# Graph attention and expert layer on one core: tile numbers turned on TensorE, x loaded first, tiles ranked, expert results scattered plainly into two halves and joined at the end

## The chip, the cores and the metric

The kernel runs on one core of one Trainium2 chip. The metric is the device time of one execution in microseconds (us); lower is better. The engines of the core are PE (TensorE, with its weight loads shown as PEld), DVE (VectorE), ACT (ScalarE), POOL (GpSimd) and SP (SyncE, which here only starts DMAs). Each engine works through its own instructions in order, and they wait for each other with semaphores.

## The reference, cut to what matters

6250 nodes with 256 features, 200000 edges sorted by destination. Two graph attention layers (4 heads, then 1), added to x, then a mixture of 8 experts of which each node takes its best two.

```python
def _gat_layer(x, src, dst, W, a_src, a_dst, b, heads, concat):
    h = (x @ W).reshape(n, heads, -1)
    e = jax.nn.leaky_relu(al_s[src] + al_d[dst], NEG_SLOPE)
    ex = jnp.exp(e - m[dst])                      # m: maximum per destination
    alpha = ex / (denom[dst] + 1e-16)             # denom: sum of ex per destination
    out = jax.ops.segment_sum(h[src] * alpha[:, :, None], dst, num_segments=n)
...
x = x + gnn(_layernorm(x), ...)                   # two such layers, elu between them
# ffn of _layernorm(x): probs = softmax(xf @ gate_w + gate_b); top 2 of 8 experts
cw = zeros((N, 8)).at[arange(N)[:, None], top2_idx].add(top2_vals)
for each expert:  h = gelu(xf @ w1 + bb1); y = h @ w2 + bb2; acc = acc + we[:, None] * y
return x + acc
```

## The kernel before

The 6250 nodes are 49 tiles of 128 rows (NT = 49), the last of which has 106 (LAST). The 200000 edges are cut into windows of 128. An item is one window for one node tile; ITEMS = 1616 items are worked off in STEPS = 202 steps of 8. The phases follow one another, each in a block of its own that all engines leave together.

**start_phase.** For each node tile SP loads a tile of x into one of SETS = 4 places of `xt`, DVE norms it (`begin_norm`, `end_norm`), PE turns it (`turn_tile`) and multiplies it by the weights (`multiply`), ACT copies the product into `acc` and POOL stores it into a table in DRAM. Between the tiles stands the edge plan. SP first copies `dst` and `src` into DRAM tables of windows, and reads the first node number of each window into `first`. At t = PLAN_AT = 2 DVE folds the second layer's weights and runs `make_plan` in one piece: how many windows begin below each tile (`below`, `count`, summed on PE), where each tile's windows begin and end, and from a comparison over 13 x 49 numbers (`cmp`) each item's tile (`tile_i`) and window (`win_i`), with items in the order of the tile numbers. SP stores `tile_i` to DRAM in 13 transfers of one column each, 128 numbers of 4 bytes, after the load for tile 6. POOL gathers the windows of 128 items at a time (`raw`), and at every third tile from t = 6 (BLOCK_AT) DVE, PE and ACT turn such a block.

**edge_phase** (twice). In a step POOL gathers 8 times 128 table rows by source node, DVE, ACT and PE weigh them and sum them by destination, and DVE adds each item's sum to its tile of `acc`. Steps run over the items in the order of the plan.

**route_norm_phase, route_phase.** The node values after the graph layers (`mid_tile`) are stored to DRAM into the later part of the tensor `back`, normed values stay in `acc`. The best two experts of each node give it two slots. POOL sends each node's row of `acc` twice to the slots' rows of the DRAM tensor `sent`: 256 values, the row number of its home in `back`, and its share (the gate's weight).

**expert_phase.** 106 slot tiles (SLOT_TILES) of 128 rows, each of one expert. SP loads a tile (`xe`); PE turns it (`turn_x`), multiplies it with the expert's first weights (`up`), turns the result (`turn_h`) and multiplies again (`down`). In PE's order tile k's `turn_h` is followed by `down` of tile k - 1. `up` and `down` begin with reading the number of the tile's expert from SBUF into a register (`value_load`, line 1595), from which the weights' address is worked out. DVE adds the biases (`bias_h`, `bias_y`), copies (`copy_h`), and finds the homes and shares (`find_home`, in rings of 8 columns). ACT does gelu (`gelu`, line 1720), copies the turned x (`copy_x`, 1716) and multiplies the result by the share (`weigh_y`, 1726). In ACT's order `weigh_y` of tile k - 1 stands between `copy_x` of tile k + 2 and `gelu` of tile k + 1. POOL scatters each result tile to its homes in `back` with a DMA that adds to what is there; each such store waits for the one before it to have landed, as a node has two.

**combine_phase.** One DMA copies 6250 rows of `back` to the output.

## Time and profile before

| | |
|---|---|
| runs of the kernel before | 5241.19, 5238.65, 5240.36 us; median 5240.36 |
| the profiled execution | 5236.12 us, with a span of 5234.5 us in the trace |
| start phase | 0 to about 125 us |
| first edge phase | about 160 to 2290 us |
| second edge phase | about 2420 to 4355 us |
| routing | about 4355 to 4680 us |
| expert phase | about 4687 to 5206 us |
| the copy to the output | 5212.4 to 5234.5 us |
| busy, of the span | PE 69%, POOL 65%, DVE 65%, ACT 28% |

A busy share over the whole span says little here, since the phases have different limits: within a phase one asks which engine never waits for long, and what ends the waits of the others. DMA work is not an engine's busy time. The chain of work that ended last is given at the end of the page; here it names PE's matmuls of the expert phase.

### The profile page before, as it was taken

The numbers are of one execution on the slowest core, as the hardware profiler recorded it, in microseconds if no ns is written. First come the engines' busy times: TensorE is split into PE (matmuls) and PEld (weight loads), VectorE is DVE, ScalarE is ACT, GpSimd is POOL, SyncE is SP. The second block draws the span as 40 slices with busy tenths as digits, with TensorE's granted clock in tenths as the row PEclk, the third lists the DMA queues.
The fourth block names the chain that finished last, engine by engine and source line by source line (L and its number), as shares of the span: only waits on it lengthen the run. The fifth ranks groups of instructions, "written<-read, shape, count | busy, mean of one in ns | idle before, by whom it ended". The sixth has DMA issues, their size and how long they took to land. (4 is left out here: it accounts for less than half of the span.)

```text
span 5234.5 us, 76220 instructions
## 1 busy us (share of the span) xinstructions
PE 3631.5 (69%) x12542; PEld 2230.4 (43%) x12543; DVE 3422.5 (65%) x8917; ACT 1488.3 (28%) x3315; POOL 3424.8 (65%) x3626
## 2 busy tenths in 40 slices
PE   5477777777777777757777777777777774219996
PEld 4244444444444444434444444444444443206664
DVE  5677777777777777776777777777766776504442
ACT  3222222222222222342222222222222222103232
POOL 4577777777777777537777777777777772353332
PEclk8677777777777878777777777777777776559998
DMA  5344444444444444325555555555555555123334
GB/s 138 108 132 132 133 133 132 133 133 134 133 133 132 133 133 133 94 90 139 138 138 139 138 138 139 139 139 139 139 138 138 139 136 162 69 79 56 55 56 87
DMA packets 298785, 644.90 MB, mean 123 GB/s; under 512 B 74539, under 2 KB 132779, under 8 KB 298322
## 3 DMA queue, kind: packets, MB, share of 16 engines
q0 software_dynamic: 183376, 475.89, 34.8%
q1 hardware_dynamic: 106882, 156.45, 10.8%
q10 hardware_dynamic: 8480, 12.06, 0.7%
q14 instruction: 34, 0.28, 0.0%
q8 instruction: 13, 0.21, 0.0%
HBM read 583.32 MB, written 68.80 MB: 125 GB/s over the span
## 5 line engine op out<-in xcount | busy, mean ns | idle before, releaser
L999 POOL DMA_INDIRECT rows<-table,idx x3232 | 3055.9, 946 | 1025.7 <-issue 919.8
L1072 PE MATMUL bank<-rows,hit 128*128 128x260 f32 (+1 forms) x6464 | 2620.7, 549 | 1080.7 <-DVE acc L1134 1065.3
L1072 PEld LDWEIGHTS bank<-rows,hit 128*128 128x128 f32 x6464 | 1467.1, 256 | 2031.7 <-DVE acc L1134 1778.2
L1134 DVE TENSOR_TENSOR acc<-acc,bank 128x260 f32 (+1 forms) x3232 | 1356.0, 420 | 180.4 <-issue 34.9
L1125 DVE TENSOR_TENSOR rows<-rows,bank 128x1024 f32<-128x1024 f32 x808 | 946.3, 1212 | 1.3 <-ACT rows L1032 1.3
L1029 ACT ACTIVATE arg<-arg 128x32 f32<-128x32 f32 (+1 forms) x404 | 88.4, 219 | 2833.7 <-DVE arg L1118 2833.7
L1111 DVE TENSOR_TENSOR arg<-rows,bank 128x32 f32<-128x32 f32 (+1 forms) x404 | 71.6, 177 | 999.9 <-DMA rows<-table,idx 999.9
L1092 DVE TENSOR_TENSOR hit<-bank,dst_loc 128x256 f32<-128x256 f32 x1616 | 672.9, 417 | 0.1
L1023 ACT ACTIVATE hit_t<-gap,ones 128x1024 bf16<-128x1024 bf16 x404 | 464.0, 1148 | 20.7
L1018 ACT ACTIVATE gap<-loc,minus_node 128x1024 bf16<-128x1024 bf16 x404 | 462.6, 1145 | 10.2 <-DMA loc<-loc_row 6.3
L1061 PE MATMUL bank<-du,hit_t 128*128 x3232 | 375.1, 184 | 119.6 <-ACT hit_t L1023 80.0
L1061 PEld LDWEIGHTS bank<-du,hit_t 128*128 128x128 bf16 x3232 | 297.6, 103 | 344.0 <-issue 253.0
L1585 POOL DMA_INDIRECT back<-ye,xe_home x106 | 163.9, 1546 | 352.6 <-ACT ye L1726 240.0
L1631 PE MATMUL bank<-fw,hidt 128*128 x848 | 212.2, 394 | 30.7 <-issue 30.6
L1612 PE MATMUL bank<-fw,xet 128*128 x424 | 206.1, 609 | 1.6 <-ACT xet L1716 1.6
L1631 PEld LDWEIGHTS bank<-fw,hidt 128*128 128x128 f32 x848 | 153.6, 191 | 71.9 <-issue 54.9
L1677 DVE TENSOR_TENSOR ye<-bank,fb 128x256 f32<-128x256 f32 x106 | 45.0, 425 | 179.5 <-PE bank L1631 179.5
L1663 DVE TENSOR_TENSOR hid<-bank,fb 128x512 f32<-128x512 f32 x106 | 73.3, 692 | 125.9 <-PE bank L1612 125.9
L1602 PE MATMUL bank<-ident,xe 128*128 128x128 f32 x212 | 40.8, 275 | 155.2 <-DMA xe<-sent 155.2
L1726 ACT ACTIVATE ye<-ye,xe_share 128x256 f32<-128x256 f32 x106 | 53.8, 508 | 315.1 <-DVE ye L1677 315.1
L1439 POOL DMA_INDIRECT sent<-acc,slot x98 | 95.6, 976 | 59.1 <-issue 29.2
L1246 POOL DMA_DIRECT2D back<-mid_tile x49 | 26.5, 541 | 143.4 <-DVE mid_tile L1266 143.4
(200 smaller groups left out, 1976.8 us busy)
## 6 DMA issues: line engine op xcount, KB each, us to landing
loc<-loc_row SPq DMA_DIRECT2D x404, 256.0 KB, 3.5
rows<-table,idx POOLq DMA_INDIRECT x3232
sent<-zeros SPq DMA_DIRECT2D x202, 68.5 KB
xe<-sent SPq DMA_DIRECT2D x106, 129.0 KB, 2.0
fw<-in_L_ffn_W ACTq DMA_DIRECT2D x16, 512.0 KB, 10.6
table<-acc POOLq DMA_DIRECT2D x49, 130.0 KB
table<-acc POOLq DMA_DIRECT2D x49, 128.5 KB, 2.4
back<-mid_tile POOLq DMA_DIRECT2D x49, 128.0 KB, 2.1
```

The costliest lines, as they stand in the source:

```text
L999: pool.indirect_dma_start(rows[:, way, n, 0:R], None, table, bass.IndirectOffsetOnAxis(idx[:, way, n:n + 1], 0)).then_inc(rows_in[way], 16)
L1018: nc.scalar.activation(gap[:, :], loc[:, way % 2, :], ACT.Abs, bias=kp.minus_node[:, 0:1]).then_inc(gap_ready, 1)
L1023: nc.scalar.activation(hit_t[:, way % 2, :, :].rearrange("p n e -> p (n e)"), gap[:, :], ACT.Relu, bias=kp.ones[:, 0:1], scale=-1.0).then_ ...
L1061: last = nc.tensor.matmul(du_bank[way % 2][:, n * 6 * H:(n + 1) * 6 * H], hit_t[:, way % 2, n, :], eb.du3[:, t, :, 0:2 * H], start=True, s ...
L1072: nc.tensor.matmul(sum_bank[n % 4][:, 0:R], hit[:, way, n, :], rows[:, way, n, 0:R], start=True, stop=True).then_inc(summed, 1)
L1092: nc.vector.tensor_tensor(hit[:, way, some, :], col.unsqueeze(1).to_broadcast([P, PAIR, P]), eb.dst_loc[:, bass.ds(s * ST + pair * PAIR, P ...
L1125: nc.vector.tensor_tensor(r, r, weight[:, some, :].unsqueeze(3).to_broadcast([P, PIECE, H, D // H]), ALU.mult).then_inc(scaled, 1)
L1134: nc.vector.tensor_tensor(kp.acc[:, t, 0:R], kp.acc[:, t, 0:R], sum_bank[n % 4][:, 0:R], ALU.add).then_inc(added, 1)
L1439: pool.indirect_dma_start(kp.sent, bass.IndirectOffsetOnAxis(fb.slot[0:few, a, t:t + 1], 0), kp.acc[0:few, t, 0:D + 2], None).then_inc(tok ...
L1585: pool.indirect_dma_start(kp.back, bass.IndirectOffsetOnAxis(home[:, way:way + 1], 0), ye[:, way % 2, :], None, compute_op=ALU.add).then_i ...
L1612: last = nc.tensor.matmul(kp.bank[2 + j][:, :], xet[:, j, c * P:(c + 1) * P], fb.w1[:, e, c, :], start=(c == 0), stop=(c == 1))
L1631: last = nc.tensor.matmul(kp.bank[6 + j][:, 0:D], hidt[:, j, c * P:(c + 1) * P], fb.w2[:, e, c, :], start=(c == 0), stop=(c == HC - 1))
```

## The change

Start phase: the loads of x for the first four tiles stand ahead of the window copies in SP's order. The plan is in three parts: `count_windows` at t = 2, `rank_tiles` at t = 4, `place_items` at t = 6; the second weights are folded at t = 0, and the blocks begin at t = 8. `rank_tiles` compares all 49 tiles with each other (49 x 49 numbers on each partition) and puts them in the order of their numbers of windows, the fewest first; the items then follow that order. It also writes the order itself to `tile_order`, which the code of the edge phases, unchanged but for a narrower tile of zeros, does not read. The items' tile numbers (`tile_f`, 128 x 13) are turned on PE, copied by ACT, and stored by one DMA of 13 rows of 512 bytes. The last tile of x has a place of its own.

From the routing on: rows of `sent` have no share. A node's second row carries a home that lies 49 tiles further on, so that `back` has a half for first results and a half for second ones, and each home is written once. Node values go to a DRAM tensor of their own (`mid_x`). In the expert phase `weigh_y` and the share's copy are gone, the stores are plain and don't wait for each other, the ring of homes has 4 columns instead of 8, and SP loads `mid_x` tile by tile into `acc` beside the first 49 slot tiles. The combine phase loads both halves tile by tile (98 loads by SP, 7 tiles deep), ACT multiplies the second by its share, DVE multiplies the first by its share and adds it, then adds the second, and POOL stores 49 tiles to the output.

```diff
-    PLAN_AT = 2
-    BLOCK_AT = [6 + 3 * blk for blk in range(BLOCKS)]
+    COUNT_AT, RANK_AT, ITEMS_AT = 2, 4, 6
+    BLOCK_AT = [8 + 3 * blk for blk in range(BLOCKS)]
...
-                    if t == PLAN_AT + 4:
-                        sp.wait_ge(win_ready, 1)
-                        for blk in range(BLOCKS):
-                            sp.dma_start(kp.tile_row[blk:blk + 1, :].rearrange("o p -> p o"), tile_i[:, blk:blk + 1]
-                                         ).then_inc(tile_written, 16)
+                    if t == ITEMS_AT + 5:
+                        sp.wait_ge(tile_kept, 1)
+                        sp.dma_start(kp.tile_row[:, :], tile_i[:, :]).then_inc(tile_written, 16)
...
+                    done.then_wait(nc.vector.scalar_tensor_tensor(key[:, :], length[:, :], 8192.0, low[:, 0:NT],
+                                                                  ALU.mult, ALU.add))
+                    done.then_wait(tt(less[:, :, :], key[:, :].unsqueeze(1).to_broadcast([P, NT, NT]),
+                                      key[:, :].unsqueeze(2).to_broadcast([P, NT, NT]), ALU.is_lt))
+                    done.then_wait(nc.vector.tensor_reduce(rank[:, :], less[:, :, :], AX.X, ALU.add))
+                    done.then_wait(tt(less[:, :, :], less[:, :, :],
+                                      length[:, :].unsqueeze(1).to_broadcast([P, NT, NT]), ALU.mult))
+                    done.then_wait(nc.vector.tensor_reduce(begin[:, :], less[:, :, :], AX.X, ALU.add))
...
-                    if not number(k) or k >= 1:
-                        pool.wait_ge(y_out[1 - way % 2], (turn * (RING // 2) + (way + 1) // 2) * 16)
-                        pool.reg_add(due, due, 0)
                     pool.indirect_dma_start(kp.back, bass.IndirectOffsetOnAxis(home[:, way:way + 1], 0),
-                                            ye[:, way % 2, :], None, compute_op=ALU.add).then_inc(y_out[way % 2], 16)
+                                            ye[:, way % 2, :], None).then_inc(y_out[way % 2], 16)
...
-                def weigh_y(k, way):
-                    act.wait_ge(y_summed, k + 1)
-                    act.wait_ge(share_ready, k + 1)
-                    y = ye[:, way % 2, :]
-                    nc.scalar.activation(y, y, ACT.Copy, scale=share[:, way:way + 1]).then_inc(y_ready, 1)
...
-                sp.dma_start(out[:, :], kp.back[SLOT_TILES * P:SLOT_TILES * P + N, :]).then_inc(stored, 16)
-                sp.wait_ge(stored, 16)
+                def load(t, j, turn):
+                    if not number(t) or t >= SETS:
+                        sp.wait_ge(ready, t - SETS + 1)
+                    for a in range(2):
+                        sp.dma_start(got[0:few(t), j, a, :], kp.back[bass.ds((t + a * NT + SLOT_TILES) * P, few(t)), :]).then_inc(got_in[j], 16)
...
+                def add(t, j, turn):
+                    m = kp.acc[0:few(t), t, 0:D]
+                    dve.wait_ge(got_in[j], (turn + 1) * 32)
+                    nc.vector.scalar_tensor_tensor(m, got[0:few(t), j, 0, :], fb.pick[0:few(t), t, 0:1], m, ALU.mult, ALU.add
+                                                   ).then_inc(added, 1)
+                    dve.wait_ge(weighed, t + 1)
+                    dve.wait_ge(added, t + 1)
+                    nc.vector.tensor_tensor(m, m, got[0:few(t), j, 1, :], ALU.add).then_inc(ready, 1)
```

SP's queue at the start of the program, before; `xt<-in_x` are the loads of x, `tile_row` the tile numbers:

```order
L323 DMA dst_windows<-in_dst 16x12496
L325 DMA dst_windows<-in_dst 16x4
L327 DMA src_windows<-in_src 16x12496
L329 DMA src_windows<-in_src 16x4
L333 DMA src_windows<-pad_src 1x64
L334 DMA src_windows<-pad_src 1x640
L333 DMA dst_windows<-pad_dst 1x64
L334 DMA dst_windows<-pad_dst 1x640
L321 DMA xt<-in_x 128x256 x4
L340 DMA first<-dst_windows 112x1792
L321 DMA xt<-in_x 128x256 x3
L346 DMA tile_row<-tile_i 128x1 x13
```

and now, the same queue:

```order
L333 DMA xt<-in_x 128x256 x4
L338 DMA dst_windows<-in_dst 16x12496
L340 DMA dst_windows<-in_dst 16x4
L342 DMA src_windows<-in_src 16x12496
L344 DMA src_windows<-in_src 16x4
L348 DMA src_windows<-pad_src 1x64
L349 DMA src_windows<-pad_src 1x640
L348 DMA dst_windows<-pad_dst 1x64
L349 DMA dst_windows<-pad_dst 1x640
L352 DMA first<-dst_windows 112x1792
L333 DMA xt<-in_x 128x256 x8
L357 DMA tile_row<-tile_i 13x128
```

The four loads of x moved to the front, and 13 stores of a column became one store, five loads of x later.

DVE in the start phase, before: the end of `make_plan`, which stands in one piece between two tiles' norms.

```order
L411 SCALAR_TENSOR_TENSOR end<-length,zero 128x49
L414 TENSOR_TENSOR off<-c,end 128x49
L417 TENSOR_TENSOR cmp<-end,item 128x637
L419 TENSOR_REDUCE tile_f<-cmp 128x13
L420 CAST tile_i<-tile_f 128x13
L421 TENSOR_SCALAR low_of<-tile_f 128x13
L422 TENSOR_TENSOR cmp<-low_of,low 128x637
L424 TENSOR_TENSOR cmp<-cmp,off 128x637
L426 TENSOR_REDUCE win_f<-cmp 128x13
L427 TENSOR_TENSOR win_f<-win_f,item 128x13
```

DVE now, in the middle of `rank_tiles` at t = 4; `place_items` follows two tiles later:

```order
L424 SCALAR_TENSOR_TENSOR key<-length,low 128x49
L426 TENSOR_TENSOR less<-key 128x2401
L428 TENSOR_REDUCE rank<-less 128x49
L429 TENSOR_TENSOR less<-less,length 128x2401
L431 TENSOR_REDUCE begin_item<-less 128x49
L432 TENSOR_TENSOR end<-begin_item,length 128x49
L433 TENSOR_TENSOR off<-start,begin_item 128x49
L435 TENSOR_TENSOR less<-rank,col 1x2401
L437 TENSOR_TENSOR less<-less,col 1x2401
L438 TENSOR_REDUCE order_f<-less 1x49
L439 CAST tile_order<-order_f 1x49
```

Seven instructions over 2401 numbers per partition are new (a reduction is printed by its result), three of them on one partition.

ACT in the loop of the expert phase, before; `hid` is gelu, `xet` the copied x, `ye` the weighing:

```order
L1726 ACTIVATE ye<-ye,xe_share 128x256
L1719 REGISTER_ALU
L1720 ACTIVATE hid<-hid 128x512
L1713 REGISTER_ALU
L1716 COPY xet<-bank 128x256
L1726 ACTIVATE ye<-ye,xe_share 128x256
```

and now, a whole turn of two tiles:

```order
L1765 ACTIVATE hid<-hid 128x512
L1758 REGISTER_ALU
L1761 COPY xet<-bank 128x256
L1764 REGISTER_ALU
L1765 ACTIVATE hid<-hid 128x512
L1758 REGISTER_ALU
L1761 COPY xet<-bank 128x256
```

The weighing of the finished result no longer stands ahead of the next tile's gelu.

## Rows read from the trace of the kernel before

**Rows 1.** Groups of instructions: line engine op names xcount, busy, mean | idle, releasers.

```profile
L999 POOL DMA_INDIRECT rows<-table,idx x3232 | 3055.9, 946 | 1025.7 <-issue 919.8
```

**Rows 2.** DVE in time: start us, length, line, op, names, [idle before, releaser].

```profile
26.49 0.17 DVE L401 CAST firstf<-first 112x14 f32<-112x14 int32 x1
...
35.47 0.42 DVE L373 BATCH_NORM_STATS2 st<-xt 128x6 f32<-128x256 f32 x1
...
52.98 0.43 DVE L373 BATCH_NORM_STATS2 st<-xt 128x6 f32<-128x256 f32 x1 [16.00 <-DMA xt<-in_x]
...
54.26 0.42 DVE L373 BATCH_NORM_STATS2 st<-xt 128x6 f32<-128x256 f32 x1
```

**Rows 3.** SP's queue in time, the same stretch.

```profile
35.59 6.02 SPq L346 DMA_DIRECT2D tile_row<-tile_i  x13
```

**Rows 4.** Groups by line: a small and a large operation of DVE.

```profile
L917 DVE TENSOR_TENSOR acc<-acc,ws 128x12544 f32<-128x12544 f32 x2 | 26.4, 13216 | 0.0
...
L417 DVE TENSOR_TENSOR cmp<-end,item 128x637 f32<-128x637 f32 x1 | 0.8, 825 | 0.0
```

**Rows 5.** DMA issues: names, engine, xcount, KB each, median us to landing.

```profile
raw<-dst_windows,win_i POOLq DMA_INDIRECT x13, 3.0
```

**Rows 6.** PE in time, first tiles of the expert phase and its last.

```profile
4700.01 0.60 PE L1621 MATMUL bank<-ident,hid 128*128 128x128 f32 x4
4700.44 1.89 PE L1631 MATMUL bank<-fw,hidt 128*128 x8
...
4704.11 0.60 PE L1621 MATMUL bank<-ident,hid 128*128 128x128 f32 x4
...
5192.55 5.40 PE L1631 MATMUL bank<-fw,hidt 128*128 x16 [0.20 <-issue]
```

**Rows 7.** All engines in time, one tile in the middle of the expert phase.

```profile
4993.22 0.69 DVE L1663 TENSOR_TENSOR hid<-bank,fb 128x512 f32<-128x512 f32 x1 [1.09 <-PE bank L1612]
...
4996.18 0.43 DVE L1677 TENSOR_TENSOR ye<-bank,fb 128x256 f32<-128x256 f32 x1 [1.67 <-PE bank L1631]
...
4996.64 0.51 ACT L1726 ACTIVATE ye<-ye,xe_share 128x256 f32<-128x256 f32 x1 [2.94 <-DVE ye L1677]
...
4997.12 0.63 ACT L1720 ACTIVATE hid<-hid 128x512 f32<-128x512 f32 x1
...
4997.94 0.60 PE L1621 MATMUL bank<-ident,hid 128*128 128x128 f32 x4
...
4998.85 1.99 PE L1631 MATMUL bank<-fw,hidt 128*128 x8 [0.31 <-issue]
```

**Rows 8.** One line's instructions: xcount, duration ns min/median/max, first and last start.

```profile
L1595 PEldq TENSOR_LOAD <-expert_of x212: 296/302/312, 4690.1 to 5193.1; - x106
```

**Rows 9.** DMA issues, the two kinds of scatter: xcount, median us to landing.

```profile
back<-ye,xe_home POOLq DMA_INDIRECT x106, 3.8
sent<-acc,slot POOLq DMA_INDIRECT x98, 2.6
```

**Rows 10.** POOL and SP in time, the end of the program.

```profile
5201.95 1.54 POOL L1585 DMA_INDIRECT back<-ye,xe_home  x1 [2.82 <-DMA back<-ye,xe_home]
5212.36 0.57 SPq L1751 DMA_DIRECT2D out<-back  x1
```

**Rows 11.** SP's queue in time, four issues in a row.

```profile
5.18 2.41 SPq L321 DMA_DIRECT2D xt<-in_x  x4
```

**Rows 12.** Stretches: length, PE, PEld, DVE, ACT, POOL busy (x), PEclk, DMA share, GB/s.

```profile
4440.00:4500.00 60.00, 32.14 (x139) 28.56 (x138) 54.20 (x210) 22.55 (x69) 12.85 (x24) 0.50 0.29 98
...
60.00:110.00 50.00, 46.61 (x224) 30.85 (x222) 44.58 (x195) 35.05 (x157) 39.72 (x55) 1.00 0.73 211
```

**Rows 13.** Groups by line: DVE's multiply and add on 256 columns.

```profile
L1263 DVE SCALAR_TENSOR_TENSOR mid_pre<-acc,mid_share,mid_bias 128x256 f32<-128x256 f32 x49 | 23.6, 482 | 12.5 <-DMA mid_xt<-in_x 10.1 <-issue 1.8
```

**Rows 14.** SP and DVE in time, around the last tile of x.

```profile
111.52 1.54 SPq L321 DMA_DIRECT2D xt<-in_x  x2
...
117.67 0.43 DVE L373 BATCH_NORM_STATS2 st<-xt 128x6 f32<-128x256 f32 x1 [1.75 <-DMA xt<-in_x]
```

More of the change, by code:

```diff
@@ L142, in build @@
             eb.wx2 = eb.sb("wx2", [P, 2, D + 2], F32)
+            eb.order = eb.sb("tile_order", [1, NT], I32)
             eb.seg = eb.sb("seg", [P, NT + 1, HEADS], F32)
@@ L320, in load @@
                     few = LAST if t == NT - 1 else P
-                    sp.dma_start(xt[0:few, t % SETS, :], x[t * P:t * P + few, :]).then_inc(x_in[t % SETS], 16)
+                    sp.dma_start(xt[0:few, place(t), :], x[t * P:t * P + few, :]).then_inc(x_in[t % SETS], 16)
+                sp.wait_ge(xt_zeroed, 1)
+                for t in range(SETS):
+                    load(t)
                 sp.dma_start(kp.dst_win[0:main, :], dst[0:main * W].rearrange("(a b) -> a b", b=W)).then_inc(
@@ L335, in _ @@
                                  pad[0:1, W - rest:]).then_inc(windows_written, 16)
-                sp.wait_ge(xt_zeroed, 1)
-                for t in range(SETS):
-                    load(t)
                 sp.wait_ge(windows_written, 8 * 16)
@@ new lines, in rank_tiles @@
+                    same = less[0:1, :, :]
+                    done.then_wait(tt(same, rank[0:1, :].unsqueeze(1).to_broadcast([1, NT, NT]),
+                                      kp.col[0:1, 0:NT].unsqueeze(2).to_broadcast([1, NT, NT]), ALU.is_equal))
+                    done.then_wait(tt(same, same, kp.col[0:1, 0:NT].unsqueeze(1).to_broadcast([1, NT, NT]), ALU.mult))
+                    done.then_wait(nc.vector.tensor_reduce(order_f[:, :], same, AX.X, ALU.add))
+                    done.then_wait(nc.vector.tensor_copy(eb.order[:, :], order_f[:, :]))
@@ L1745, in combine_phase @@
         b = kp.within(ctx)
+        SETS = 7
+        got = b.sb("got", [P, SETS, 2, D], F32)
+        got_in = [b.sem(f"got_in{j}") for j in range(SETS)]
+        weighed = b.sem("second_weighed")
+        added = b.sem("first_added")
+        ready = b.sem("out_ready")
         stored = b.sem("out_stored")
+        few = lambda t: LAST if number(t) and t == NT - 1 else P
+        at = lambda t, rows: slice(t * P, t * P + rows) if number(t) else bass.ds(t * P, P)
         with nc.Block() as block:
```

158 lines of the change are left out of this document (103 added, 55 removed).

## Prediction, made before the changed kernel had run

> **What bounds the kernel now.** The two edge phases are four fifths of the span, so I read them first, in the groups by line: POOL's 3232 gathers are busy for 3055.9 us and idle for 1025.7 more, of which 919.8 is its own issuing [rows 1]. POOL is the pace there, at (3055.9 + 919.8) / 3232 = 1.23 us a gather, and the change leaves gathers, steps and their number alone. What can move is the start phase, the expert phase and what follows it, and each has another limit. In the start phase, DVE in time shows two losses: the plan, from 26.49 to 35.47, and a wait of 16.00 us for x right behind it [rows 2]. SP's queue says why: 13 stores of tile numbers are issued from 35.59 to 41.61, and the next loads of x are queued behind them [rows 3]. Otherwise DVE goes from tile to tile in 54.26 - 52.98 = 1.28 us [rows 2] and hardly waits. In the expert phase PE hardly waits either, yet it loses time: the first `down` begins at 4700.44 and the 105th at 5192.55 [rows 6], 492.1 / 104 = 4.73 us a tile, while the first turn of all four pieces, from `turn_h` at 4700.01 to the next at 4704.11, took 4.10 us [rows 6]. The end is one copy of 22.1 us, from 5212.36 [rows 10] to the span's end at 5234.5.
>
> **Start phase.** Removed: the wait of 16.0 us [rows 2]. One store of 13 rows of 512 bytes takes the place of 1664 numbers of 4 bytes, and SP reaches it with five more loads of x issued. Added: DVE's work. Between 825 ns for 637 numbers and 13216 ns for 12544 [rows 4] lies 1.04 ns a number, so 2401 numbers cost 0.825 + 1764 x 0.00104 = 2.66 us. `rank_tiles` has seven of these (18.6 us; those on one partition are taken to cost the same) and seven small ones of about 0.25, together 20.4 us. `place_items` has seven of 637 numbers (5.8) and six small ones, 7.3 us. `count_windows` keeps about 2.0 us. That makes 29.7 us where the plan took 9.0 [rows 2]: +20.7. A wait comes too: the first block now follows `place_items` by two tiles (2.6 us), and needs two gathers, some 1.6 us of POOL's issuing and 3.0 us to land [rows 5], so DVE stands still for about 2.0 to 2.5 us. Before, the 16 us hid that. Having x first gains about 0.7 us, for behind it ACT is busy issuing the attention weights' loads in both. Nothing covers the plan's work, as DVE is the limit there. Sum: 20.7 - 16.0 + 2.3 - 0.7 = +6.3; range +3 to +11, the upper end if PE, idle for 20 us during the ranking, then works a few tiles at its lower clock.
>
> **Edge phases.** Items in another order are the same gathers of random rows: 0. I allow 0.1% of 4100 us, 4 us, either way.
>
> **Routing.** One copy of 49 columns leaves DVE's path (0.2 us): 0.
>
> **Expert phase.** Where do the 0.63 us go? In the middle of the phase, `hid` has its bias at 4993.22 + 0.69 = 4993.91, and its gelu starts only at 4997.12 [rows 7]. In between stands, in ACT's order, the weighing of an earlier result, which waited for DVE's `ye` at 4996.18 [rows 7]. `turn_h` follows gelu at 4997.94, and `down` 0.91 us later with 0.31 us of PE idle, put down to issue [rows 7]. In the first turn, where no weighing was due yet, it followed after 0.43 us with none [rows 6]. So PE's sequencer, held at `turn_h` until gelu is done, has not begun to read the next expert's number: a read of 0.30 us [rows 8] and the address work behind it then lie bare, and the sequencer's lead is used up. Without `weigh_y` gelu can end near 4994.6, three microseconds before PE needs it; the sequencer runs ahead, and the turn is 4.10 us. What is late next: DVE has about 2 us of work (0.69 for `hid`, 0.43 for `ye` [rows 7], a copy like the first and a short `find_home`) and two reads of the expert's number in a turn, the second between `find_home` and `bias_h`, with about 0.2 us to spare. ACT and SP have room. I take 4.10: 104 x (4.73 - 4.10) = -65.5. Bounds: if the 0.31 us stays, 4.41 and -33; if the time is lost elsewhere, 0. SP puts a load of `mid_x` ahead of the second slot tile's: +0.4. The other 48 are hidden, with a turn of 4.1 us and three transfers of 128 KB in it.
>
> **Its end.** Now the last store starts 4.0 us after PE's end (5192.55 + 5.40 to 5201.95) [rows 6, 10], as it waits for the add before it. Without that wait and the weighing it starts about 1.4 us after. A plain scatter lands in 2.6 us, the adding one in 3.8 [rows 9]. Together 2.6 + 1.2 = -3.8.
>
> **Combine phase.** 98 loads and 49 stores of 128 KB stand where one copy took 22.1 us. Three paces: SP issues four loads in 2.41 us [rows 11], 0.60 each, 98 are 59 us. The bytes are 12.8 + 6.4 = 19.2 MB; the DMA engines moved 98 GB/s at a share of 0.29 and 211 at 0.73 [rows 12], 338 or 289 GB/s when full, so 57 or 66 us. DVE needs 0.48 for the multiply-add [rows 13] and 0.43 for the add, 46 us. ACT, with 0.51 a tile [rows 7], is hidden. I take 60 us, near the first two since loads and stores are the kinds of the 0.29 row. Then the drain: the last tile has 106 rows, and the last load of x, issued by 111.52 + 1.54 = 113.06, let DVE go at 117.67 [rows 14], 4.6 us. Two of them, then DVE, the store's issue and its landing: 5 to 7 + 1 + 3, about 10. Total 70, so +48; bounds 60 and 85 us, +38 and +63.
>
> The Trainium skill ("DMA: Bandwidth & Descriptors", on why a DMA increments its semaphore by 16) states that a transfer is spread over the largest number up to 16 that divides its rows, so 106 rows go over 2 engines. By this both last loads share the same two, and the drain is nearer 7 than 5 us for them. The wait of 1.75 us for this tile [rows 14] agrees. The same page, under "Issuing engines are not separate DMA queues", has POOL's stores run on the engines of SP's loads. By that rule the 6.4 MB count; without it the loads' bytes need 38 us at 338 GB/s and issue alone sets the pace, 59 instead of 60.
>
> **Sum.** 6.3 - 65.5 + 0.4 - 3.8 + 48 = -14.6 us. The profiled execution took 5236.12 us, its span 5234.5, and lies 4.2 us below the median of the three runs. The difference is taken off the median: 5240.36 - 14.6 = 5226 us, and by its own parts 5212 to 5240.
>
> **Rivals.** *The combine costs more.* If loads and stores disturb each other, the full rate is 289 GB/s or less, and the drain comes on top: 81 to 85 us, +60, in all 5238. For it: the 0.73 row, of a stretch with many kinds at once. Against it: that stretch has 256 and 512 byte pieces. *The combine costs less*, 60 us: 5216, if issue runs below 0.5 us and all paces fall together.
> *The gap on PE stays.* The reads come twice a turn in any case [rows 8]; if they, and not gelu, bare the 0.31 us, a turn is 4.41 and the phase gives 33 us instead of 65: 5259, slower. The first turn speaks against it, though it is not yet loop code with its register arithmetic.
> *The shorter ring binds.* `find_home` of tile k + 2 now waits for the store of tile k - 2, not k - 6. From it to the result of tile k DVE needs about 2.9 us, and a store about 1.3 us to be issued after its result, so two turns last at least 2.9 + 1.3 + landing. That reaches 8.2 us when a landing takes 4.0 us. At 5.0 us a turn is 4.6: 65 - 104 x 0.13 leaves 14 us, 5278, slower. Plain scatters of the routing land in 2.6 us [rows 9].
> *The change doesn't do what it says:* the rank gives a shorter or longer edge phase, though nothing there reads `tile_order`. At 0.3% of a phase's 2100 us either way this is 6 us; at 1%, 41 us for both, of either sign.
>
> **Chances.** Forecast 0.56; combine dearer 0.18; cheaper 0.08; gap stays 0.09; ring 0.05; edge phases 0.04. What a measurement of this kernel can tell from no change is about 0.2%, 10.5 us: faster is below 5230, slower above 5251. Of the forecast's 0.56, 0.43 lies below 5230; with the cheap combine and small parts of the others, faster is 0.53. Slower is the gap, the ring and half the edge case, with a little of the dear combine: 0.17. The rest, 0.30, is within. The range 5208 to 5260 holds the forecast, both combines and the gap, and leaves out the ring and the edge case.
>
> **What would show it.** Start: no wait for `xt` behind one `tile_row` store, seven DVE rows of 2.66 us, a wait for `raw` of 2 us, and the last norm about 6 us later than now. Expert phase: gelu directly behind `hid`, no issue gap before `down`, turns of 4.10 us; a DVE wait at `find_home` for the scatter would be the ring. Combine: SP's issues 0.6 us apart and a DMA share near 1 for 60 us, 70 in all. The forecast is wrong if the turn stays above 4.3 us, or if the combine lasts beyond 85.

## The result, and the profile after

The changed kernel took 5219.16 us (median of 6 runs, 5216.99 to 5222.06) beside 5239.50 us of the kernel before (6 runs on the same chip). The ratio is 0.9961, with a 95% interval of 0.9948 to 0.9973: 20 us faster, where 5226 and a range of 5208 to 5260 had been predicted. The profiled execution has a span of 5217.2 us, 17.3 less than the 5234.5 before. These runs and the one with half-wide loads below belong to occasions on which the kernel before took about 5240 us; on those of all other experiments it took 6375 to 6494 us, because the two edge phases took 2576 to 2651 us each instead of 2019, in every kernel alike.

Three groups of the page after, with line, engine, operation, names and count, then busy us, mean ns, and the idle time before them. They answer to [rows 1], to the `down` of [rows 6] and to the stores of [rows 10].

```profile
L1042 POOL DMA_INDIRECT rows<-table,idx x3232 | 3055.7, 945 | 1025.7 <-issue 925.0
...
L1631 POOL DMA_INDIRECT back<-ye,xe_home x106 | 101.7, 959 | 342.1 <-DVE xe_home L1732 337.1
...
L1677 PE MATMUL bank<-fw,hidt 128*128 x848 | 200.5, 379 | 0.0
```

The gathers are the same to 0.2 us in 3056, ranked or not. PE's `down` has no idle time ahead of it any more, and between 4700 and 5120 us PE is busy for 419.1 of 420 us. A store is on POOL for 959 ns, where the adding one in [rows 10] took 1.54 us.

**Start phase.** DVE in time (start, length, line, operation, names, idle before). The first two rows are the first and the last of the seven large operations of `rank_tiles`; they answer to [rows 2], the last two to [rows 14].

```profile
31.23 2.66 DVE L426 TENSOR_TENSOR less<-key 128x2401 f32<-128x2401 f32 x1
...
47.86 2.64 DVE L438 TENSOR_REDUCE order_f<-less 1x49 f32<-1x2401 f32 x1
50.54 0.18 DVE L439 CAST tile_order<-order_f 1x49 int32<-1x49 f32 x1
50.75 0.43 DVE L383 BATCH_NORM_STATS2 st<-xt 128x6 f32<-128x256 f32 x1
...
64.31 0.25 DVE L464 CAST val<-raw 128x128 f32<-128x128 int32 x1 [1.44 <-DMA raw<-dst_windows,win_i]
...
121.30 0.43 DVE L383 BATCH_NORM_STATS2 st<-xt 128x6 f32<-128x256 f32 x1 [2.13 <-DMA xt<-in_x]
...
123.58 0.43 DVE L383 BATCH_NORM_STATS2 st<-xt 128x6 f32<-128x256 f32 x1 [0.32 <-DMA xt<-in_x]
```

No row behind the plan waits 16 us for x; what came is the ranking, from 30.28 to 50.75. The last norm starts at 123.58, where it was 117.67 in [rows 14]: 5.9 us later. Three parts of the change bear on the wait that went (x loaded first, the store five loads later, 13 stores turned into one); no run separates them. SP's queue shows one store of tile numbers where [rows 3] has thirteen:

```profile
13.02 39.46 SPq L333 DMA_DIRECT2D xt<-in_x  x8
58.70 0.33 SPq L357 DMA_DIRECT2D tile_row<-tile_i  x1
```

**Expert phase.** All engines in time, a tile in the middle, to be laid beside [rows 7]:

```profile
4901.92 0.69 DVE L1709 TENSOR_TENSOR hid<-bank,fb 128x512 f32<-128x512 f32 x1 [1.06 <-PE bank L1658]
...
4902.64 0.63 ACT L1765 ACTIVATE hid<-hid 128x512 f32<-128x512 f32 x1 [0.25 <-DVE hid L1709]
...
4905.92 0.60 PE L1667 MATMUL bank<-ident,hid 128*128 128x128 f32 x4
...
4906.36 1.89 PE L1677 MATMUL bank<-fw,hidt 128*128 x8
```

Gelu starts 0.03 us after `hid` has its bias (4901.92 + 0.69), not 3.2 us after it. It is done at 4903.27, 2.65 us before PE turns its result, and `down` follows `turn_h` after 0.44 us with no gap. The instructions of `down`, with count, duration in ns (min/median/max), first and last start:

```profile
L1677 PE MATMUL bank<-fw,hidt x848: 379/379/462, 4705.4 to 5133.1; 128*128 x170
```

That is 427.7 us for 105 turns, 4.07 us each (the last tile's other seven matmuls, 1.5 us, are counted in, here and in every kernel below; by the same count the kernel before has 4.73). From the first `down` to PE's end the phase went from 497.5 to 428.0 us, 69.5 less.

**Its end and the combine phase.** POOL and SP in time, and POOL's DRAIN, with which it leaves the block (an instruction of its sequencer; count, duration in ns three times, start):

```profile
5134.80 0.96 POOL L1631 DMA_INDIRECT back<-ye,xe_home  x1 [0.77 <-DVE ye L1723]
5146.40 54.22 SPq L1799 DMA_DIRECT2D got<-back  x98
...
L1594 POOLq DRAIN  x1: 8711/8711/8711, 5137.4 to 5137.4; - x1
```

The same row of the kernel before:

```profile
L1553 POOLq DRAIN  x1: 6302/6302/6302, 5205.8 to 5205.8; - x1
```

The last scatter has landed by 5137.4, and POOL then needs 8.71 us to leave the block, 2.41 us more than before. So from PE's end (5133.45) to SP's first load 12.95 us pass, where 14.4 passed before: the quicker store and landing gained 3.9 us, the DRAIN took 2.4 of it back.

The combine phase: a stretch of 50 us (length, then PE, PEld, DVE, ACT, POOL busy, PEclk, DMA share, GB/s), SP's loads as one row, and the program's end in time.

```profile
5150.00:5200.00 50.00, 0.00 (x0) 0.00 (x0) 37.66 (x87) 21.85 (x44) 23.33 (x43) 0.50 0.99 333
...
L1799 SPq DMA_DIRECT2D got<-back x98: 292/333/642, 5146.4 to 5200.0; - x98
...
5204.43 0.54 POOL L1807 DMA_DIRECT2D out<-acc  x1 [0.51 <-DVE acc L1831]
5209.29 0.51 ACT L1817 ACTIVATE got<-got,pick 106x256 f32<-106x256 f32 x1 [5.67 <-DMA got<-back]
...
5210.60 0.61 POOL L1807 DMA_DIRECT2D out<-acc  x1 [5.63 <-DVE acc L1831]
```

98 loads went out in 54.2 us. Then 8.7 us passed until the last tile's two loads, of 106 rows, let ACT and DVE go, and 7.9 us more until the end at 5217.2. Together 70.8 us, where the copy took 22.1.

**The account.** The first `down` is 5.0 us later, the expert phase 69.5 us shorter, its end 1.45 shorter, the combine 48.7 longer: 5.0 - 69.5 - 1.45 + 48.7 = -17.3 us, the whole difference of the spans. The edge phases are nothing in it: from the first to the last gather they took 2018.9 and 2018.9 us before, 2019.0 and 2018.6 after. (Before, these gathers run from 160.4 to 2179.3 and from 2315.2 to 4334.1 us. For the two inner times the table ahead of the prediction has 2290 and 2420.)

### The profile page after: what moved, and what is told of

Same layout as the page of the kernel before. It is cut to its first block and busy times, and to the rows that moved or that the text cites. A ratio compares the mean times of both kernels' runs of the same rounds, so it can differ in the third digit from the quotient of the medians.

```text
span 5217.2 us, 76931 instructions
## 1 busy us (share of the span) xinstructions
PE 3597.0 (69%) x12543; PEld 2228.6 (43%) x12544; DVE 3484.7 (67%) x8919; ACT 1470.6 (28%) x3259; POOL 3389.5 (65%) x3675
## 5 line engine op out<-in xcount | busy, mean ns | idle before, releaser
L1631 POOL DMA_INDIRECT back<-ye,xe_home x106 | 101.7, 959 | 342.1 <-DVE xe_home L1732 337.1
L1677 PE MATMUL bank<-fw,hidt 128*128 x848 | 200.5, 379 | 0.0
L1761 ACT COPY xet<-bank 128x256 f32<-128x256 f32 x106 | 39.6, 374 | 462.1 <-PE bank L1648 462.1
L1677 PEld LDWEIGHTS bank<-fw,hidt 128*128 128x128 f32 x848 | 152.9, 190 | 16.6
L1648 PEld LDWEIGHTS bank<-ident,xe 128*128 128x128 f32 x212 | 29.9, 142 | 211.8 <-issue 211.0
```

The source lines that it names most:

```text
L1631: pool.indirect_dma_start(kp.back, bass.IndirectOffsetOnAxis(home[:, way:way + 1], 0), ye[:, way % 2, :], None).then_inc(y_out[way % 2], 16)
L1677: last = nc.tensor.matmul(kp.bank[6 + j][:, 0:D], hidt[:, j, c * P:(c + 1) * P], fb.w2[:, e, c, :], start=(c == 0), stop=(c == HC - 1))
```

## The experiments

Each run is compared with runs of the kernel before on its own chip, and what an edit did to a stage is read from that stage, as the long edge phases differ by some us from trace to trace. "A turn" is the time from one tile's `down` to the next.

### Where the 0.66 us a turn came from

**Weighing back on ACT.** The changed kernel, with one ACT operation per result where `weigh_y` had stood. It multiplies by 1.0; stores stay plain.

```diff
+                def weigh_y(k, j):
+                    act.wait_ge(y_summed, k + 1)
+                    nc.scalar.activation(ye[:, j, :], ye[:, j, :], ACT.Copy, scale=1.0).then_inc(y_ready, 1)
...
                     if not number(k) or k + 2 < T:
                         copy_x(k + 2, j)
+                    if not number(k) or k >= 1:
+                        weigh_y(k - 1, 1 - j)
```

> The changed kernel with an ACT operation on every result again, in the place that weigh_y had in ACT's order (between copy_x of tile k + 2 and gelu of tile k + 1), multiplying by 1.0; plain stores, two halves and the combine phase stay. Theory (the weighing ahead of gelu holds PE's sequencer at turn_h and bares the read of the expert's number): a turn goes from 4.10 to about 4.7 us, down has an issue gap of 0.3 us again, and the whole is some 60 to 65 us longer than the changed kernel, about 5282. Rival (the gain came from plain stores that don't wait for each other): the turn stays at 4.10 and the whole within 3 us of the changed kernel's 5219.

Measured: 1.0060 of the kernel before (1.0038 to 1.0081). The row of `down`, and a tile in time:

```profile
L1678 PE MATMUL bank<-fw,hidt x848: 379/379/478, 5949.5 to 6437.2; 128*128 x170
...
6184.61 0.42 DVE L1724 TENSOR_TENSOR ye<-bank,fb 128x256 f32<-128x256 f32 x1 [1.64 <-PE bank L1678]
...
6185.07 0.42 ACT L1770 ACTIVATE ye<-ye 128x256 f32<-128x256 f32 x1 [2.91 <-DVE ye L1724]
...
6185.39 0.62 ACT L1766 ACTIVATE hid<-hid 128x512 f32<-128x512 f32 x1
...
6186.26 0.60 PE L1668 MATMUL bank<-ident,hid 128*128 128x128 f32 x4
...
6187.14 1.99 PE L1678 MATMUL bank<-fw,hidt 128*128 x8 [0.28 <-issue]
```

487.7 / 105 = 4.64 us a turn: plain stores and all, nearly the whole loss is back, and so is the gap ahead of `down`. From the first `down` to PE's end the phase takes 488.1 us, 60.1 more than in the changed kernel, as expected. The remaining 0.09 us to 4.73 is what this ACT operation is shorter than the old one (0.42 against 0.51 us) in the same chain: `ye`, weighing, gelu, `turn_h`. That is a fit of numbers and not shown; the plain stores could have a part in it. The rival, that plain stores alone made the gain, falls.

**The same without PE's reads.** Gelu is as late as in the run above, but PE does not read the expert's number: every tile is multiplied by expert 0's weights, so that the address work behind the read is gone too.

```diff
                 def up(k, j, pair):
...
-                    e = expert(k)
+                    e = 0
...
                 def down(k, j, pair):
...
-                    e = expert(k)
+                    e = 0
```

> The kernel with the weighing put back on ACT ahead of gelu (a turn of 4.65 us), and PE's two reads of the expert's number per tile left out: every tile is multiplied by the first expert's weights, so only the time is of use. Gelu is as late as in that kernel; only the reads are gone. Theory (what costs is the reads that lie bare once PE's sequencer has been held at turn_h): the turn falls back to 4.10 to 4.25 us. Rival (the late gelu itself makes PE wait, the reads don't matter): the turn stays at 4.5 to 4.65.

```profile
L1678 PE MATMUL bank<-fw,hidt x848: 379/379/382, 5936.5 to 6367.5; 128*128 128x256 f32 x170
...
6066.68 0.42 ACT L1770 ACTIVATE ye<-ye 128x256 f32<-128x256 f32 x1 [2.54 <-DVE ye L1724]
...
6067.00 0.61 ACT L1766 ACTIVATE hid<-hid 128x512 f32<-128x512 f32 x1
...
6067.73 0.60 PE L1668 MATMUL bank<-ident,hid 128*128 128x128 f32 x4
...
6068.16 1.89 PE L1678 MATMUL bank<-fw,hidt 128*128 128x256 f32 x8
```

431.0 / 105 = 4.10 us. Gelu still stands directly behind the weighing and ends 0.12 us before `turn_h`, yet the turn is back to that of the changed kernel. The whole took 0.9972 (0.9957 to 0.9987). So it takes both: the late gelu, which holds PE's sequencer, and the reads with their address work, which then have nothing to hide behind (how much of it is the read and how much the addresses was not separated). The late gelu alone costs 0.03 us; the reads alone, in the changed kernel, leave no idle time ahead of `down`.

**Only the order changed, in the kernel before.** Adding stores that wait for each other and the one copy at the end stay.

```diff
                     gelu(k, way % 2)
+                    if not number(k) or k >= 2:
+                        weigh_y(k - 2, (way + RING - 2) % RING)
                     if not number(k) or k + 2 < T:
                         copy_x(k + 2, way % 2)
-                    if not number(k) or k >= 1:
-                        weigh_y(k - 1, (way + RING - 1) % RING)
```

> The kernel before with one change: in ACT's order the weighing of tile k - 2 stands behind gelu of tile k and ahead of copy_x, where before the weighing of tile k - 1 stood behind copy_x; the adding stores that wait for each other stay, and so does the one copy at the end. Theory: PE's gap goes, and what is late next is the chain of stores, of which one takes 1.54 us on POOL and lands before the next is issued; the distance of the last two stores was 4.37 us, so a turn of 4.4 to 4.5 us and 25 to 35 us off the kernel before, about 5210. Rival (stores and their waits made the 4.73): the turn stays at 4.73, no gain. Rival (the reads bare the gap in any order): also 4.73, with 0.3 us of issue ahead of down.

Measured: 0.9984 (0.9973 to 0.9995), some 10 to 12 us where 25 to 35 had been expected, and 476.9 / 105 = 4.54 us a turn. POOL's stores (first and last start), the waits, summed over the phase (us in total, times, longest), and one of them in time:

```profile
L1585 POOL DMA_INDIRECT back<-ye,xe_home x106: 1542/1545/1643, 5956.1 to 6440.1; - x106
...
DVE ye L1677 <- DMA back<-ye,xe_home: 183.4, 93, 2.8
...
6181.66 0.42 DVE L1677 TENSOR_TENSOR ye<-bank,fb 128x256 f32<-128x256 f32 x1 [1.78 <-DMA back<-ye,xe_home]
```

PE's gap ahead of `down` is gone, and a new wait has come: DVE stands ahead of `ye` until the store two tiles back has landed. The order alone takes 0.2 us off PE's turn, but not off the phase: the stores follow each other at (6440.1 - 5956.1) / 105 = 4.61 us, and the last one leaves 10.5 us after PE's end instead of 4.0. From the first `down` to the last store the phase is 13.8 us shorter (487.8 against 501.5), 0.13 us a turn. This explains the small gain: the chain of adding stores is the next limit, 4.61 us and not the expected 4.4 to 4.5. Only with plain stores is the gain 0.66.

### What the ranking costs

The changed kernel with items in the order of the tile numbers; `tile_order` is not computed.

```diff
-                    done.then_wait(nc.vector.scalar_tensor_tensor(key[:, :], length[:, :], 8192.0, low[:, 0:NT],
-                                                                  ALU.mult, ALU.add))
...
-                    done.then_wait(tt(end[:, :], begin[:, :], length[:, :], ALU.add))
+                    done.then_wait(nc.vector.tensor_tensor_scan(end[:, :], length[:, :], zero[:, :], 0.0, ALU.add,
+                                                                ALU.add))
+                    done.then_wait(tt(begin[:, :], end[:, :], length[:, :], ALU.subtract))
```

> The changed kernel without the ranking: items in the order of the tile numbers by a running sum as in the kernel before, and tile_order, which nothing reads, is not computed; tile numbers are still turned on PE and stored by one DMA. Theory: ranking costs its seven operations of 2.65 us and four small ones on DVE, about 19.5 us, of which nothing is hidden, and the order of the items makes no difference to the edge phases (2018.9 us from first to last gather in both): about 5200. Rival (the ranks help the edge phases, which a saved start would give back): more than 5205. Rival (part of the work was hidden by waits for x and raw): 5204 to 5212.

Measured: 0.9942 (0.9919 to 0.9964). DVE at the last tile of x, and POOL's gathers (first and last start):

```profile
104.90 0.43 DVE L380 BATCH_NORM_STATS2 st<-xt 128x6 f32<-128x256 f32 x1 [2.23 <-DMA xt<-in_x]
...
L1028 POOL DMA_INDIRECT rows<-table,idx x3232: 941/949/1191, 148.0 to 5570.9; - x191
```

The last norm starts 18.7 us earlier than in the changed kernel, the first gather at 148.0 instead of 166.9. From the first to the last gather the two edge phases took 2639.5 and 2646.8 us, and with ranked items in the run of one block below 2640.0 and 2644.2: the order of the items bought nothing that these traces could show, and the traces of 2019 us leave it no more than 0.4 us. The ranking is a plain loss of 19 us here, and without it the new start phase is 12.8 us shorter than the old one (104.90 against 117.67).

### The way into the combine phase

The expert and combine phases in one block, so that no engine leaves a block in between.

```diff
+                for j in range(2):
+                    sp.wait_ge(y_out[j], 16 * (T // 2))
+                steps(sp, NT, load, SETS)
...
                 steps(pool, T, store, RING)
-                for j in range(2):
-                    pool.wait_ge(y_out[j], 16 * (T // 2))
```

> The changed kernel with the expert phase and the combine phase in one block: SP waits for the last scatters itself and starts the loads of both halves at once, POOL does not end a block in between. In the changed kernel POOL ends its block with a DRAIN of 8.71 us after the last scatter has landed (from 5137.44), and the first load goes out at 5146.40. Theory: nothing else holds the loads, so 9 us less, about 5210. Rival (the DRAIN shows work of POOL that the loads or the stores to the output need, such as descriptors of the scatters): the time comes back as a wait of the first stores on POOL, but as the loads set the pace the end moves by less than 3 us. Rival (loads that start at once meet the last scatters' traffic): also less.

Measured: 0.9939 (0.9917 to 0.9961). POOL's last scatter and SP's first load:

```profile
6385.32 0.96 POOL L1649 DMA_INDIRECT back<-ye,xe_home  x1 [0.77 <-DVE ye L1747]
6387.79 2.24 SPq L1629 DMA_DIRECT2D got<-back  x5
```

2.5 us instead of 11.6. The phase itself took 71.5 us instead of 70.8, so 8.4 of the 9.1 us stayed. The DRAIN did no work that the loads waited for.

### What sets the combine phase's pace

**Half as wide.** The second results' loads carry 128 of 256 columns; as many transfers, 16.05 instead of 19.2 MB.

```diff
+                        wide = D if a == 0 else D // 2
-                        sp.dma_start(got[0:few(t), j, a, :], kp.back[bass.ds((t + a * NT + SLOT_TILES) * P, few(t)), :]).then_inc(got_in[j], 16)
+                        sp.dma_start(got[0:few(t), j, a, 0:wide],
+                                     kp.back[bass.ds((t + a * NT + SLOT_TILES) * P, few(t)), 0:wide]
+                                     ).then_inc(got_in[j], 16)
```

> The changed kernel with the loads of the second results half as wide (128 of 256 columns, the rest is zero), so that part of the result is missing; the number of loads and stores and the work of DVE and ACT stay. Theory (the bytes set the combine phase's pace): 16.05 instead of 19.2 MB at 333 GB/s are 48 us, 9.5 us less, so the phase goes from 70.8 to 61 to 62 us. Rival (the number of transfers or their issuing on SP sets it): it stays at 70 us. Rival (a row of 512 bytes costs as much as one of 1024): also 70.

Measured: 5218.7 us, 0.9956 of the kernel before (0.9937 to 0.9976), the same as the changed kernel. The same stretch and SP's loads:

```profile
5150.00:5200.00 50.00, 0.00 (x0) 0.00 (x0) 36.53 (x84) 21.33 (x42) 22.24 (x41) 0.50 0.84 276
...
L1801 SPq DMA_DIRECT2D got<-back x98: 332/333/497, 5148.7 to 5202.3; - x98
```

My theory fell. The DMA share went from 0.99 to 0.84 and the loads still took 53.6 us from first to last, as in the changed kernel; the phase took 69.1 us, 1.7 less. The rival with the rows of 512 bytes falls as well: had they cost as much as 1024, the share would have stayed at 0.99. 53.6 / 97 = 0.55 us is what SP needs per load: 0.33 to 0.34 for the issue, about 0.10 for register instructions, and the rest shows no instruction.

**Two queues.** ACT issues the second results' loads.

```diff
+                    if t >= SETS:
+                        act.wait_ge(ready, t - SETS + 1)
+                    act.dma_start(got[0:few(t), j, 1, :],
+                                  kp.back[(t + NT + SLOT_TILES) * P:(t + NT + SLOT_TILES) * P + few(t), :]
+                                  ).then_inc(got_in[j], 16)
```

> The changed kernel with the loads of the second results issued by ACT instead of SP, six tiles ahead of the weighing, so that each queue issues 49 instead of SP all 98. Theory (the bytes set the pace of the combine phase: its DMA share is 0.99 at 333 GB/s, and 19.2 MB at that rate are 57.6 us): the phase stays at 70 to 72 us and the whole is that of the changed kernel. Rival (SP's issuing, 54.2 us for 98 loads, sets it): 8 to 15 us less, until DVE's 46 us are the limit. Rival (ACT's issues delay its weighing): a few us longer.

Measured: 0.9990 (0.9975 to 1.0005), the phase 77.9 us. SP's loads now span 61 us, and DVE waits for ACT:

```profile
L1798 SPq DMA_DIRECT2D got<-back x49: 271/333/432, 6304.1 to 6365.2; - x49
...
6366.25 0.43 DVE L1842 TENSOR_TENSOR acc<-acc,got 128x256 f32<-128x256 f32 x1 [0.73 <-ACT got L1823]
```

ACT's load of a later tile stands ahead of its weighing and waits for DVE, which waits for the weighing: SP's loads come 1.38 us apart, one for each tile. This run tells nothing on whether issue or bytes set the pace; it has a wait of its own. From the other two: SP issues at 0.55 us a load whatever the bytes, and the DMA engines are full at 0.99. Fewer bytes alone gained 1.7 us. What fewer issues alone would gain is open: 19.2 MB at 333 GB/s are 57.7 us, no less than SP's 54.2, so my estimate is little; a version that relieves SP without a new wait was not run.

**The end of the phase.** The last tile's loads are split into 96 and 10 rows, and ACT stores to the output instead of POOL.

```diff
+                        for lo, n in ((0, 96), (96, LAST - 96)) if few(t) == LAST else ((0, P),):
+                            sp.dma_start(got[lo:lo + n, j, a, :],
...
-            @block.gpsimd
...
+                for t in range(NT):
+                    weigh(t, t % SETS, t // SETS)
+                    if t >= 1:
+                        store(t - 1)
```

> The changed kernel with two edits in the combine phase: the loads of the last tile (106 rows) are split into 96 and 10 rows each, and the stores to the output are issued by ACT instead of POOL. Theory: if the long wait for the last tile (5.16 us on DVE, against 0.0 to 0.9 for the others) comes from its two loads running on few DMA engines, it falls to 1 to 2 us; and POOL's DRAIN of 4.04 us behind its last store leaves the end of the program, as ACT's drains take under 0.6 us. Together 6 to 8 us less than the changed kernel. Rival (the last loads wait only behind the queued bytes): the wait stays at 5 us, 4 us less in all. Rival (the DRAIN is a fixed price of a block's end, whoever stores): neither gains, 0.

Measured: 0.9984 (0.9968 to 1.0001), the phase 63.7 us instead of 70.8.

The first row is the changed kernel's wait for its last tile (a stretch, columns as above), the others are this run's.

```profile
5206.00:5208.00 2.00, 0.00 (x0) 0.00 (x0) 0.00 (x0) 0.00 (x0) 0.00 (x0) 0.50 0.13 50
```

```profile
L1800 SPq DMA_DIRECT2D got<-back x100: 318/333/513, 6296.0 to 6350.7; - x100
...
6354.30 0.51 ACT L1810 ACTIVATE got<-got,pick 106x256 f32<-106x256 f32 x1 [0.91 <-DMA got<-back]
6354.30 0.48 DVE L1829 SCALAR_TENSOR_TENSOR acc<-got,pick,acc 106x256 f32<-106x256 f32 x1 [0.39 <-DMA got<-back]
6354.31 1.56 ACTq L1815 DMA_DIRECT2D out<-acc  x2
```

From the last load's issue to the last multiplication 3.6 us pass instead of 9.3, although the bytes are the same. The Trainium skill ("DMA: Bandwidth & Descriptors", on why a DMA increments its semaphore by 16) says that a transfer goes over the largest number up to 16 that divides its rows, which makes two for 106 and sixteen for 96. The runs agree: near the end of the changed kernel's wait the DMA share is 0.13, as much as two of 16 engines make, and with the split loads it stays at 0.99 or more up to 6354. From DVE's last instruction (5209.88, 6354.89) to the end it is 4.8 us instead of 7.3: the DRAIN of 4.04 us is gone, but the way from the last issue's start to the DRAIN grew from 2.3 us with POOL to 4.1 with ACT (5210.60 to 5212.93, 6355.35 to 6359.48). In all 7.1 us of stages, within the 6 to 8 expected; both edits ran together, and their shares are read from the trace.

### The best of each side

**The changed kernel with four edits:** no ranking, one block, the split loads and ACT's stores. It ran twice.

> The changed kernel with four edits together: no ranking, one block for the expert and combine phases, the last tile's loads split, stores to the output from ACT. Theory (they lie one behind the other on the path): 19 to 21 for the ranking, 9 for the block, 6 to 8 for the end, 34 to 38 us less than the changed kernel and about 1% less than the kernel before. Rival (ACT, with its own stores in the same block, starts its weighing late): 5 us less of that.

> The changed kernel as it is, beside its best variant on one chip. 0.3 to 0.5% below the kernel before; combine phase 70.8 us, first load 10.6 us after the last scatter's issue.

> The changed kernel without the ranking, with one block for the expert and combine phases, the last tile's loads split and the output stored from ACT. By its stages 19.4 us for the start, 9.1 for the block and 7.1 for the end, together 35.6 us less than the changed kernel: 0.7% less than it where that takes 5219 us, 0.55% where the edge phases are slower.

Measured: 0.9921 (0.9893 to 0.9949), then 0.9909 (0.9894 to 0.9925) beside the changed kernel's 0.9975 (0.9963 to 0.9987): 6422.4 against 6463.3 us on one chip, 40.9 us or 0.6% less, where 35.6 were expected. In the two traces, everything outside the edge phases differs by just 35.6 us (1179.8 against 1144.2), and the edge phases, which no edit touches, by 9.2. Where the edge phases take 2019 us, 5219 - 36 = 5183 us would be my estimate; it was not run there.

**The kernel before with four edits:** the weighing behind the next gelu, four buffers of `ye`, the new start phase without the ranking, the copy issued in the expert phase's block.

```diff
-        ye = b.sb("ye", [P, 2, D], F32)
+        ye = b.sb("ye", [P, 4, D], F32)
...
-                    if not early(k):
-                        dve.wait_ge(y_out[j], pair * 16)
+                    if not number(k) or k >= 4:
+                        dve.wait_ge(y_out[j], (pair - 1) * 16)
```

> The kernel before with adding stores and one copy at the end, but with: the weighing behind the next gelu in ACT's order, four buffers of ye instead of two, the changed kernel's start phase without the ranking, and the copy to the output issued in the expert phase's block. Theory: with four buffers DVE no longer waits for a store to land before ye, and the chain of stores alone sets the turn, 4.37 us between the last two before, so 4.37 to 4.42 instead of 4.54; the start phase ends 12 to 13 us earlier than before, the copy starts 9 us earlier, and the whole is 55 to 60 us less than the kernel before, the same as the changed kernel with its four edits. Rival (landings stretch as stores follow each other closer): a turn of 4.5 and 45 us less.

Measured: 0.9935 (0.9914 to 0.9956), 34 us less than the kernel before where 55 to 60 had been expected. POOL's stores (first and last start), PE's `down`, and a store in time:

```profile
L1616 POOL DMA_INDIRECT back<-ye,xe_home x106: 1542/1545/1646, 5843.6 to 6328.3; - x106
...
L1660 PE MATMUL bank<-fw,hidt x848: 379/379/478, 5839.7 to 6307.9; 128*128 x170
...
6107.18 1.54 POOL L1616 DMA_INDIRECT back<-ye,xe_home  x1 [3.09 <-DMA back<-ye,xe_home]
```

PE came down to 4.46 us a turn, but the stores follow each other at (6328.3 - 5843.6) / 105 = 4.62 us, as in the run with only the order changed, not at the 4.37 that I had taken from the last two of the kernel before; the last store left 20 us after PE was done. 106 adding stores, each waiting for the one before, take 484 to 485 us in both runs, however early their results are. The two halves lift that limit and pay for it in the combine phase, 49 us in the changed kernel. On one chip the times of the two best versions lie within each other's intervals, 0.9921 and 0.9935, so the whole time does not decide between them. The stages do: from the first `down` to the end it is 534.1 us in the kernel before, 514.8 in its best variant, and 495.3 and 495.5 in the two runs of the changed kernel's. So once both sides have their cheap edits, the two halves are worth about 19 us.

## Why the prediction was right, point by point

**Start phase, +6.3: +5.9 at the last norm.** The seven operations took 2.64 to 2.66 us against 2.66 expected, on one partition too; `place_items` took 6.7 us, not 7.3. PE's granted clock did fall, as the upper end of the range had it: 0.57 of full speed while the ranking ran (PE was busy for 0.75 of 19.7 us), 0.50 (1.2 GHz) from 50.7 to 60 us and 0.78 to 70. The last norm was no later for it than the sum says, and the kernel before shows the same level, 0.53, from 53 to 60 us. The wait for `raw` was 1.4 us, not 2.3; the last tiles of x waited 0.7 us longer in all than before. That nothing covers the plan's work was right: without the ranking the last norm starts 18.7 us earlier.

**Edge phases, 0.** Right: at most 0.3 us in 2018.9. The rival with the rank has no support in any run.

**Expert phase, -65.5: -69.5.** The step held, and `a_weigh` and `a_noread` show both halves of it: gelu behind the weighing holds the sequencer, and the reads with their address work bare the time. 4.10 was 0.03 too much, which is 3 us of the 4. But the sum gave the whole 0.63 us to the weighing. With the kernel before's adding stores the order alone shortened PE's turn by 0.19, so the plain stores had to come with it; the prediction counted them only at the phase's end. The rival that the gap stays is out: PE reads as often as before, and its gap is gone. The ring of four homes did not bind: a store landed in 2.4 us at the median, and DVE has no wait at `find_home` after the first two tiles, which wait for their loads.

**Its end, -3.8: -1.45.** The terms were right in sum (-3.9), but a term was missing: POOL's DRAIN at the end of a block. I had read the 22.1 us of the copy and the 4 us to the last store, and not the 8.9 us between the store's end and the copy. It was in the trace before, 6.3 us, and grew by 2.4, which the prediction put at nothing.

**Combine phase, +48: +48.7, by luck: two errors cancel.** The time for the loads was 54.2 us, not 60: SP needs 0.55 us a load, not the 0.60 of four loads at the start of the program. The drain was 16.6 us, not 10: I had allowed 5 to 7 us for two loads of 106 rows, which took 8.7, and nothing for the DRAIN of 4.0 at the program's end. DVE's 46 us were a slip, 49 x (0.48 + 0.43) = 44.6; it was busy for 44.5 and set nothing. The rival of a dearer combine through DMA traffic did not come: the rate was 333 GB/s at a share of 0.99, near the 338 of [rows 12]. That the bytes set the pace beside the issue did not hold: a sixth fewer changed 1.7 us.

**Sum.** -14.6 was forecast for the median, which fell by 20.3; the profiled executions, from which the terms came, differ by 17.3. The largest step, the late gelu, is shown; the closeness of the sum also owes something to errors that partly cancel: -4.0 us in the expert phase, -1.7 ahead of it, +2.35 at its end and +0.7 in the combine phase.

## What to carry to other kernels

On an engine that works in order, an operation that waits for a late result must not stand ahead of one that another engine's sequencer waits for: 0.42 us of work on ACT ahead of gelu cost 0.57 us in each turn (4.64 against 4.07), through the reads on PE. Look at once for the limit behind the one you lift: with adding stores the same edit gained 0.13 us a turn. Price the way between two phases as a line of its own, with the landing, the DRAIN of POOL and the first issue: here it was 11.6 us from the last scatter to the first load, 8.7 of them the DRAIN. And before an order is computed for someone to use, ask who uses it: here 19 us of work on the busiest engine fed nobody.

## What the runs showed of the hardware that was not expected

POOL left these blocks with a DRAIN of 4 to 9 us that began after its last DMA had landed: 8.71 us behind plain scatters, 6.30 behind the adding ones, 4.04 at the end of the program. (The changed kernel's two edge phases show 22.3 and 22.7 us, but there the DRAIN begins 14 us before POOL's last gather has started.) The other engines' DRAINs at the end of the changed kernel's expert phase took 0.01 to 1.64 us. What sets its length was not found; one block instead of two took it off the way to the loads.

In the traces with long edge phases, short instructions of two sequencers, DVE's and SP's, take far longer than elsewhere. The register instruction ahead of DVE's add of an item's sum, in the changed kernel's first trace and in its second:

```profile
L1177 DVEq FUSED_REGOPS  x3232: 57/57/65, 190.8 to 4358.8; - x191
```

```profile
L1177 DVEq FUSED_REGOPS  x3232: 2/57/1450, 192.4 to 5616.5; - x191
```

The median is the same, but the longest went from 65 ns to 1450. DVE's idle time ahead of this add that is put down to issue went from 32 to 1119 us. Of the register, branch and semaphore instructions of the second trace, 1720 of 15610 on DVE and 389 of 2660 on SP took over 0.5 us, and none on PE, ACT or POOL. The other ten traces with long edge phases have 1456 to 1784 and 324 to 399 of them; the three with 2019 us have none on DVE and SP. So the two go together in all 14 traces. That the slow instructions make the phases long is likely, as DVE stands idle at them, but no run changed them alone; what makes them slow, and why SP's and not the others', stays open. All of the time fell on the edge phases (1256 us of the 1256 by which the two spans differ): a turn of the expert phase was 4.07 us on either.
